# One exponential for three key tiles of a softmax, and the bias matmuls moved behind the next group's first scores

## What is computed

```python
proj = x @ w_in
k, v, q = jnp.split(proj, 3, axis=-1)
scores = jnp.einsum('bhqd,bhkd->bhqk', q, k) * scale
scores = scores + _tisa_bias(amplitudes, sharpness, offsets, s)[None]
weights = jax.nn.softmax(scores, axis=-1)
attn = jnp.einsum('bhqk,bhkd->bhqd', weights, v)
```

## Time and profile before

| | us |
|---|---|
| median of 3 runs | 685.02 (679.88 to 686.0) |
| the profiled execution | 682.68 |
| its span, first to last instruction | 680.9 |

### The profile page before, as it was taken

One profiled execution on the slowest core, in us unless ns is written; L12 is line 12 of the kernel. 1 busy time (PEld: TensorE's weight loads), 2 busy tenths in 40 slices (PEclk: granted clock), 3 DMA queues, 4 the chain that ended last, 5 costly groups with the idle time before them and its releaser, 6 DMA issues.

```text
span 680.9 us, 12673 instructions
## 1 busy us (share of the span) xinstructions
PE 593.0 (87%) x3995; PEld 161.9 (24%) x3995; DVE 575.9 (85%) x698; ACT 540.8 (79%) x592; POOL 119.7 (18%) x100
## 2 busy tenths in 40 slices
PE   5791799999999999999999999999999998599411
PEld 2450121222222222222222222222222223244300
DVE  5973797999999999999999999999999993125797
ACT  2761797999999999999999999999999993013410
POOL 5730600010110101010110101011010101033355
PEclk8896797999999999999999999999999999656655
DMA  9236460625335161525435151524526104200004
GB/s 211 72 90 134 135 131 8 131 45 115 81 75 129 28 134 31 130 52 100 89 64 132 27 134 36 122 63 90 109 50 127 26 9 104 61 0 0 0 0 124
DMA packets 30191, 54.44 MB, mean 80 GB/s; under 512 B 9577, under 2 KB 21230, under 8 KB 29038
## 3 DMA queue, kind: packets, MB, share of 16 engines
q1 hardware_dynamic: 29886, 53.97, 35.3%
q10 hardware_dynamic: 288, 0.26, 0.1%
HBM read 43.86 MB, written 9.18 MB: 78 GB/s over the span
## 4 chain that ended last, share of the span: by engine, by line
ACT 37%; issue 30%; PE 7%; DVE 5%; DMA 4%; POOL 3%; SPq 1%; ACTq 1%; POOLq 0%; DVEq 0%
ACT pbuf L969 16%; ACT split L969 16%; PE ps L1155 4%; ACT pbuf L977 3%; ACT split L977 2%; DMA qb<-m_scratch 2%; DMA rd<-r_scratch 2%; DVE kb L1258 1%; PE ps L1157 1%; POOL kb L829 1%; PE ps L892 1%; DVE v_all L1255 1%; ACT o_sbs L733 1%; DVE kb L1337 1%; ACTq L968 1%
## 5 line engine op out<-in xcount | busy, mean ns | idle before, releaser
L926 DVE TENSOR_TENSOR pbuf<-ps,t 128x1024 f32<-128x1024 f32 x192 | 232.5, 1223 | 24.9 <-PE ps L867 20.4
L926 DVE TENSOR_TENSOR split<-ps,t 128x1024 f32<-128x1024 f32 x192 | 229.0, 1216 | 11.5 <-PE ps L867 6.3
L969 ACT ACTIVATE pbuf<-pbuf 128x1024 f32<-128x1024 f32 x192 | 205.4, 1236 | 24.0 <-DVE pbuf L926 23.8
L867 PE MATMUL ps<-qb,kb 64*128 64x512 f16 x1024 | 184.4, 391 | 24.2 <-SPq L793 14.4
L969 ACT ACTIVATE split<-split 128x1024 f32<-128x1024 f32 x192 | 201.0, 1245 | 0.1
L892 PE MATMUL ps<-split,vst 128*32 128x512 f32 x1024 | 137.7, 611 | 1.0 <-ACT split L977 1.0
L892 PE MATMUL ps<-pbuf,vst 128*32 128x512 f32 x1024 | 136.4, 605 | 0.0
L867 PEld LDWEIGHTS ps<-qb,kb 64*128 64x128 f16 x1024 | 48.6, 93 | 312.0 <-DVE pbuf L926 116.8
L876 PE MATMUL ps<-t64s,ident 128*64 128x512 f16 x512 | 80.2, 393 | 0.0
L977 ACT ACTIVATE split<-ps 128x1024 f32<-128x1024 f32 x64 | 77.1, 1204 | 0.0
L977 ACT ACTIVATE pbuf<-ps 128x1024 f32<-128x1024 f32 x64 | 76.6, 1197 | 0.0
(11 more groups left out here) (132 smaller groups left out, 367.5 us busy)
## 6 DMA issues: line engine op xcount, KB each, us to landing
t<-g_scratch SPq DMA_DIRECT2D x16, 960.0 KB
kb<-k_scratch SPq DMA_DIRECT2D x120, 64.0 KB
t64s<-gh_scratch SPq DMA_DIRECT2D x16, 248.0 KB
t64s<-gl_scratch SPq DMA_DIRECT2D x16, 248.0 KB
qb<-q_scratch SPq DMA_DIRECT2D x60, 64.0 KB
x_sb<-in_L_attn_x SPq DMA_DIRECT2D x4, 512.0 KB, 7.5
q_scratch<-split SPq DMA_DIRECT2D x8, 256.0 KB, 3.3
k_scratch<-split SPq DMA_DIRECT2D x8, 256.0 KB, 4.0
```

The costliest lines, as they stand in the source:

```text
L867: last = eng.matmul(ps[:, u + c, :], kb[p][rows, keys], qb[p][rows, b * HALF:(b + 1) * HALF], start=True, stop=True)
L926: eng.tensor_tensor(slot(g, b), banks(unit(k), 2), t128[p][:, t * P:t * P + S], ALU.add).then_inc(z_ready, 1)
L969: eng.activation(buf, buf, ACT.Exp).then_inc(p_ready, 1)
```

## The change

The exponentials of a group change places: ACT first takes that of the fourth tile out of PSUM, which counts a new semaphore `pd_ready` up, and then one exponential over the three tiles that DVE has written, which lie side by side (`slots`); it waits for all three adds and counts `p_ready` up once a group. ACT's half copy at a change of heads stands between the two. On PE the bias matmuls become a function of their own, `bias(i, g)`, issued one step later, behind the first scores of the next group: scores(g+2, 0), bias(g+1), products(g, 0), scores(g+2, 1), products(g, 1), scores(g+2, 2), scores(g+2, 3). The products wait for `pd_ready` and `p_ready`; the scores of batch 3 wait for `pd_ready` alone.

```diff
+        pd_ready = sem("pd_ready")
...
+        def slots(g, n):
+
+            k = 4 * (g % SETS)
+            return big[:, k * S:(k + n) * S] if k < 8 else splitf[:, (k - 8) * S:(k - 8 + n) * S]
...
-                            eng.wait_ge(p_ready, i * (8 * GPH) + 4 * g)
+                            eng.wait_ge(pd_ready, i * (2 * GPH) + g)
...
                     if by_vector:
                         last.then_inc(sd_ready, 1)
-                        return
+
+                def bias(i, g):
+
+                    p, t = (g // GPH) % 2, g % GPH
                     for c in range(2):
                         for m in range(2):
                             c0 = t * P + 64 * m + c * HALF
-                            last = eng.matmul(ps[64 * m:64 * m + 64, u + c, :], ident2[:, :],
+                            last = eng.matmul(ps[64 * m:64 * m + 64, 4 + c, :], ident2[:, :],
                                               t64[p][:, c0:c0 + HALF], start=False, stop=True,
                                               skip_group_check=True)
                     last.then_inc(sp_ready, 1)
...
                     if c == 0:
-                        eng.wait_ge(p_ready, i * (8 * GPH) + 4 * (g + 1))
+                        eng.wait_ge(pd_ready, i * (2 * GPH) + (g + 1))
+                        eng.wait_ge(p_ready, i * (2 * GPH) + (g + 1))
...
                 for g in range(LAG):
                     for b in range(B):
                         scores(0, g, b)
+                    if g < LAG - 1:
+                        bias(0, g)
                 with eng.Fori(0, NH2) as i:
                     for g in range(2 * GPH):
...
+                        if g + LAG < 2 * GPH:
+                            scores(i, g + LAG, 0)
+                            bias(i, g + LAG - 1)
+                            products(i, g, 0)
+                            scores(i, g + LAG, 1)
+                            products(i, g, 1)
+                            for b in range(2, B):
+                                scores(i, g + LAG, b)
+                            continue
...
             def _(eng):
                 with eng.Fori(0, NH2) as i:
                     for g in range(2 * GPH):
-                        for b in range(B):
-                            buf = slot(g, b)
-                            if b < DPG:
-                                eng.wait_ge(z_ready, i * (2 * DPH) + (DPG * g + b + 1))
-                                eng.activation(buf, buf, ACT.Exp).then_inc(p_ready, 1)
...
-                                eng.wait_ge(sp_ready, i * (2 * GPH) + (g + 1))
-
-                                eng.wait_ge(groups_done, i * (2 * GPH) + (g + 1))
-                                eng.activation(buf, banks(4, 2), ACT.Exp).then_inc(p_ready, 1)
...
+                        eng.wait_ge(sp_ready, i * (2 * GPH) + (g + 1))
+                        eng.wait_ge(groups_done, i * (2 * GPH) + (g + 1))
+                        eng.activation(slot(g, DPG), banks(4, 2), ACT.Exp).then_inc(pd_ready, 1)
+                        if g == LAG - 1:
...
+                        eng.wait_ge(z_ready, i * (2 * DPH) + DPG * (g + 1))
+                        eng.activation(slots(g, DPG), slots(g, DPG), ACT.Exp).then_inc(p_ready, 1)
```

More of the change, by code:

```diff
@@ L902, in _ @@
                         scores(0, g, b)
+                    if g < LAG - 1:
+                        bias(0, g)
                 with eng.Fori(0, NH2) as i:
                     for g in range(2 * GPH):
[L906 to L916, removed]
+                        if g + LAG < 2 * GPH:
[7 more added lines that the diff above has]
+                            continue
+                        if g + LAG == 2 * GPH:
+                            with eng.If(i < NH2 - 1):
+                                scores(i, g + LAG, 0)
+                            bias(i, g + LAG - 1)
+                        else:
+                            with eng.If(i < NH2 - 1):
+                                scores(i, g + LAG, 0)
+                                bias(i, g + LAG - 1)
+                        products(i, g, 0)
+                        with eng.If(i < NH2 - 1):
+                            scores(i, g + LAG, 1)
+                        products(i, g, 1)
+                        with eng.If(i < NH2 - 1):
+                            for b in range(2, B):
+                                scores(i, g + LAG, b)
             @block.vector
@@ L964, in _ @@
                     for g in range(2 * GPH):
-                        for b in range(B):
-                            buf = slot(g, b)
-                            if b < DPG:
-                                eng.wait_ge(z_ready, i * (2 * DPH) + (DPG * g + b + 1))
-                                eng.activation(buf, buf, ACT.Exp).then_inc(p_ready, 1)
-                            else:
-                                if g == SETS // 2:
-                                    eng.wait_ge(qk_out, 16 * 4 * B)
-                                eng.wait_ge(sp_ready, i * (2 * GPH) + (g + 1))
-                                eng.wait_ge(groups_done, i * (2 * GPH) + (g + 1))
-                                eng.activation(buf, banks(4, 2), ACT.Exp).then_inc(p_ready, 1)
[L978 to L987, removed]
@@ new lines, in _ @@
+                        if g == SETS // 2:
+                            eng.wait_ge(qk_out, 16 * 4 * B)
+                        eng.wait_ge(sp_ready, i * (2 * GPH) + (g + 1))
+                        eng.wait_ge(groups_done, i * (2 * GPH) + (g + 1))
+                        eng.activation(slot(g, DPG), banks(4, 2), ACT.Exp).then_inc(pd_ready, 1)
+                        if g == LAG - 1:
+                            with eng.If(i > 0):
+                                eng.wait_ge(groups_done, i * (2 * GPH) + SETS)
+                                eng.wait_ge(o_stored[1], i * (16 * B))
+                                copy_half(eng, 1, 1).then_inc(o_ready[1], 1)
@@ L988, in _ @@
+                        if g == GPH + LAG - 1:
+                            eng.wait_ge(groups_done, i * (2 * GPH) + (GPH + SETS))
+                            eng.wait_ge(o_stored[0], i * (16 * B) + 16 * B)
+                            copy_half(eng, 0, 1).then_inc(o_ready[1], 1)
+                        eng.wait_ge(z_ready, i * (2 * DPH) + DPG * (g + 1))
+                        eng.activation(slots(g, DPG), slots(g, DPG), ACT.Exp).then_inc(p_ready, 1)
                 eng.wait_ge(groups_done, H * GPH + SETS)
```

## The result

The changed kernel took 698.72 us (median of 4, 697.27 to 701.29) beside 685.51 for the kernel before; the ratio is 1.0203, 95% interval 1.0125 to 1.0282. Timed again later, beside runs of before at 680.14, it took 701.83, ratio 1.0311 (1.0263 to 1.0359). So it is slower, by 2 to 3%; neither interval reaches 1. Forecast were 690.2 and a range up to 698: the sign was right, the size was not, and the measured time lies outside the range. The profiled execution took 701.29 us.

The account below looks back on a forecast made before the run. PE's own pace, 3.75 us a group, was taken to bound the kernel, with ACT as slow. Changes of heads +3.6, end +1.0 and first head +0.6, total +5.2, gave 690.2 us on the runs' median; range 680 to 698.

Parts of the forecast that it names:

- PE's own pace: PE's order within a group: one change of matmul shape goes, so PE alone would take 3.67 us instead of 3.75.
- The loop: From the bias of g through ACT and the products to the bias of g+2: 7.49 us for two groups.
- ACT's price: The wide exponential on ACT takes 2.76 us; ACT's work falls from 3.75 to 3.56 us a group.
- L408's slope: Upper price for the wide exponential's columns on ACT, 0.93 ns each or 2.95 us in all; 0.83 was taken.
- The wait that takes the place of the old one: Products on PE wait for ACT's wide exponential, which gives back PE's 0.08 us: 3.745 us a group.
- The term ACT to PE: Step from the end of ACT's wide exponential to PE's products: 0.06 us.
- rival 2: Longer way through ACT, by a second wait's own instruction or a dearer wide exponential: about 696 us or more; chance 0.30.
- DVE's reciprocal: Once a head on DVE, costed at nothing, as it holds up an even group with 0.15 us of slack.
- The change of heads: ACT's half copy costs 0.48 us, DVE's makes scores 0.28 late: a head of 30.72, +0.24, fifteen times +3.6.
- The first head: The bias that ran ahead of PE's wait for a DMA now stands behind those scores: +0.6 us.
- The step that failed: SP's loads and the stores are not moved and their waits on groups_done keep their place; no cost was given.
- the end: The last two products, 2.87 us apart before, would be 3.83 apart: +1.0 us.

Follow-up runs that it names:

- order_only: The changed kernel with PE's new order but ACT's old one, three exponentials of 1024 columns and then the fourth: 682.14 us, ratio 1.0022 to the kernel before.
- exp_only: The kernel before with ACT's new order alone, the bias matmuls left directly behind the group's last scores: 681.91 us, ratio 1.0001 to the kernel before.
- split_swap: The kernel of after_split with the products' two waits in the other order, p_ready then pd_ready: 686.58 us, ratio 1.0100 to the kernel before.
- before_light: The kernel before with most of the load of the bias table that DVE adds left out: 681.24 us, ratio 1.0006 to the kernel before.
- after_split: The changed kernel with SP loading the next head's q and k ahead of the half-copy waits and denominators, the rest behind: 689.05 us, ratio 1.0134.
- after_again: The changed kernel unaltered, timed once more on one chip beside its version with the smaller load: 701.83 us, ratio 1.0311 to the kernel before.

## Why the prediction was wrong, step by step

- **PE's own pace:** forecast 3.67 us a group, measured 3.62. The pair of scores that follows directly came a little cheaper: six matmuls and the step to the bias are 0.75 (307.93 to 308.68), not 0.80. Held. The loop gains the same 0.05 on its way back, which hides a part of the next point's miss: 7.49 became 7.55, not 7.60.
- **ACT's price:** 2.76 us forecast, 2.76 measured; L408's slope was rightly set aside. The estimate by the Trainium skill ("ScalarE: Activation LUTs", What ACT_TABLE_LOAD costs) was 2.75, and the trace agrees with its 2.76.
- **The wait that takes the place of the old one:** the mechanism held, and order_only and exp_only fit it: each half alone costs nothing that shows. The term ACT to PE was mis-sized: 0.06, taken from scores that wait on one semaphore; it is 0.15 for products that wait on two. That is over the 0.1 that the prediction named as a sign of rival 2. split_swap moved it back to 0.06 and took 0.29 off a head, and 2.5 us off the median (a difference of two medians that each vary by as much; 15 x 0.29 = 4.4 by the heads). Rival 2 had named this mechanism and a price of the right size. That the measured 698.7 fits its "about 696 or more" is luck all the same: more of the loss came from the load than from this wait, and no rival names the load.
- **DVE's reciprocal, costed at nothing:** the scores behind it start 0.12 late (319.11 to 319.98 is 0.87 instead of 0.75), but the group after them is by as much shorter, 3.80 instead of 3.93. The slack of the even group covers it. Held.
- **The change of heads:** from the products of the last group over the first two of the new head, 297.22 to 301.19 and to 305.62, are 8.40 us; 30.72 less three loops of 7.49 left 8.25 for it. The second wait does not explain this 0.15: split_swap has 8.38 there (4.05 and 4.33 instead of 3.97 and 4.42), since what the swap gains behind ACT's half copy is lost again in front of it, where PE waits for DVE's. Its saving stands in the other three loops. Together the head without waits for DMA is 31.05, and 30.76 in split_swap, against 30.72; that the last two lie so close is in part luck, as PE's 0.05 a group is gained and this 0.15 lost.
- **The first head, forecast as +0.6:** not seen. From first products to first products it took 36.11 us before and 31.42 after. Before, PE stood 2.88 us for the load and the granted clock was 0.53 from 105 to 110 us; after, the wait was 0.46 and the clock 1.00. before_light, with the same load in its first head, took 31.97, so this varies from one execution to the next and tells nothing of the term.
- **The step that failed:** "The loads on SP and the stores are not moved, and their waits on groups_done keep their place." The words on the kernel before ("SP loads the next head's q, k and bias tables when a head's groups are done", "the change moves none of this") have the same fault. SP's load has no wait of its own on ACT, but in SP's queue it stands behind the wait for o_ready, so behind ACT's half copy. The change moved that copy behind the bias and the fourth exponential, 1.9 us later after a head's first scores by the rows above, and load and scores form a ring of 11.4 + 20.2 + 0.2 us on average, more than the 31.05 that the loop leaves. I read the ring's slack in the first head alone, where PE waited for the DMA, and took it for a matter of the start. The third head of before waited too, and the ring's 9.5 + 20.2 us stood under the head of 30.48 by less than 1 us. Price: 9.4 us by the smaller load on one chip, 11.8 by after_split as worked out below, either way more than the forecast's whole +5.2.

On the chip of after_again the loss of 21.7 us is then: 9.4 the ring, 15 x 0.29 = 4.4 the second wait, 15 x (30.76 - 30.48) = 4.2 the loop and DVE's half copy, forecast as 3.6; and 1.3 in the last head (28.79 us from its first products to the end of its last, 27.46 before), 0.7 of it at the end, forecast as 1.0, where the last two products are 3.58 apart:

```profile
580.22 1.92 PE L902 MATMUL ps<-split,vst 128*32 128x512 f32 x16 [0.28 <-ACT split L1007]
...
583.80 1.07 PE L902 MATMUL ps<-split,vst 128*32 128x512 f32 x8 [1.66 <-ACT split L1007]
```

The remaining 2.4 us are not placed. after_split, on another chip, closes the sum without them: it lost 9.9 us, and 4.4 + 4.2 + 1.3 are 9.9. By it the ring's part would be 21.7 - 9.9 = 11.8 us, and 15 x (31.83 - 31.05) = 11.7 by the heads of the trace. So the ring costs 9.4 to 11.8 us, the larger part of the miss, and the medians don't part these values.

## What to carry to other kernels

When a step is moved on one engine, follow its semaphore into every queue that waits for it, and there to all that stands behind the wait: a transfer that nobody moved can start later. For each transfer, compare in several steady turns when it lands and when it is wanted; a wait for it in the first turn is a reason to look at the others, which here had 0 to 2.5 us to spare. Where an instruction waits on two semaphores, the order in which the waits are written decides whether the late one costs an instruction more, here 0.09 us, and 0.29 over a head. And merging instructions to unload an engine lengthens each one's latency: with the bias early the wide exponential gave heads of 30.03 us, with the bias one step later 30.57, against 30.48 without it.

## What was not expected of the hardware

The two waits: 0.15 us from an exponential's end to the products when the late semaphore is waited for by an instruction of its own, 0.06 when the weight load itself waits for it. And a transfer of 16 KB issued behind some 2 MB of load kept DVE waiting until 307.96, 11 us after its issue at 296.92: moving the loads ahead of it on SP's queue made the kernel 10% slower (ratio 1.0982).
